# Dealing out a search step's maxima and a layer norm's sums, and letting GpSimd's differences run four batches behind

## What is computed

```python
# ctx_4096: (16, 1601, 2048), channel map; x: (16, 64, 2048)
k = 38                                   # of the 64 channels of x
_, topk_idx = jax.lax.top_k(cm, k)
mask = jnp.zeros((B, L, C), x.dtype).at[b_idx, l_idx, topk_idx].set(1.0)
crucial_features = crucial_channels * x
subcrucial_features = subcrucial_channels * x
c_max = jnp.max(crucial_features, axis=1, keepdims=True)
s_max = jnp.max(subcrucial_features, axis=1, keepdims=True)
...
x = x + _L0_xattn_ref(_layernorm(x, axis=-1), ctx_4096, ...)
```

## Time and profile before

| | us |
|---|---|
| median of three runs | 2584.66 (2582.23 to 2588.15) |
| profiled execution, its own time | 2591.74 |
| its span, first to last instruction | 2589.9 |
| search | 0 to 838 |
| flags, two rows done again | 838 to 916 |
| maxima stage | 916.4 to 996.7 |
| convolution, gates, attention, feed-forward | 996.7 to 2589.9 |

### The profile page before, as it was taken

How to read it: one execution, slowest core, us unless ns; L and a number is a source line. 1 busy time by engine, 2 the same in 40 slices (tenths; PEclk the granted TensorE clock), 3 DMA queues, 4 the chain that set the end, 5 groups by cost and what they waited for, 6 DMA issues and landing times. The chain is left out here.

```text
span 2589.9 us, 38980 instructions
## 1 busy us (share of the span) xinstructions
PE 2071.0 (80%) x15304; PEld 1714.1 (66%) x15304; DVE 1415.6 (55%) x2152; ACT 1023.5 (40%) x2002; POOL 968.0 (37%) x874
## 2 busy tenths in 40 slices
PE   4668678677776021558999999999999989989999
PEld 3555557566666021546887787888777767878887
DVE  5777879887888789572244464014444451651000
ACT  5665757666665023351223233222322322332222
POOL 1111111111110043266555554555554534544544
PEclk8888889888998565778999999999999999999999
DMA  8886767678884010224222444432224435434443
GB/s 323 299 302 233 274 209 273 234 259 282 284 280 144 25 65 0 77 89 151 85 82 76 153 139 125 127 98 82 78 79 158 139 98 193 139 102 131 140 153 111
DMA packets 141062, 407.67 MB, mean 157 GB/s; under 512 B 15184, under 2 KB 27728, under 8 KB 139728
## 3 DMA queue, kind: packets, MB, share of 16 engines
q1 hardware_dynamic: 140592, 403.55, 46.3%
q0 software_dynamic: 288, 1.64, 0.2%
HBM read 379.96 MB, written 25.17 MB: 156 GB/s over the span
## 5 line engine op out<-in xcount | busy, mean ns | idle before, releaser
L1059 POOL TENSOR_TENSOR t<-t,t 128x512 fp32r<-128x512 f32 (+1 forms) x488 | 643.4, 1329 | 627.6 <-ACT t L1052 627.3
L1593 PE MATMUL ps<-t,t 128*128 128x512 f32 x1856 | 744.8, 401 | 46.4 <-POOL t L1059 43.7
L1594 PE MATMUL ps<-t,t 128*128 128x512 f32 x1856 | 729.2, 393 | 0.0
L1595 PE MATMUL ps<-t,t 128*128 128x512 f32 x1856 | 729.0, 393 | 0.0
L683 PE MATMUL ps<-t,t 128*128 128x128 bf16 (+1 forms) x6656 | 486.1, 237 | 242.9 <-DVE t L435 233.8
L683 PEld LDWEIGHTS ps<-t,t 128*128 128x128 bf16 x6656 | 447.5, 109 | 314.1 <-DVE t L435 266.3
L1052 ACT ACTIVATE t<-t 128x512 fp32r<-128x512 f32 (+1 forms) x488 | 295.5, 608 | 750.7 <-PE ps L1595 478.6
L435 DVE TENSOR_SCALAR t<-t,t 128x1601 bf16<-128x1601 f32 x512 | 513.5, 1052 | 31.0 <-PE ps L683 27.1
L645 ACT ACTIVATE t<-t,t 128x1601 bf16<-128x1601 f32 x256 | 416.9, 1628 | 89.6 <-DVE t L595 84.4
L1593 PEld LDWEIGHTS ps<-t,t 128*128 128x128 f32 x1856 | 352.3, 190 | 130.2 <-POOL t L1059 36.1
L1595 PEld LDWEIGHTS ps<-t,t 128*128 128x128 f32 x1856 | 352.1, 190 | 75.7
(11 more groups left out here) (205 smaller groups left out, 1788.3 us busy)
## 6 DMA issues: line engine op xcount, KB each, us to landing
t<-ctxT SPq DMA_DIRECT2D x256, 800.5 KB, 5.7
t<-wqkv SPq DMA_DIRECT2D x192, 256.0 KB, 3.2
t<-wo SPq DMA_DIRECT2D x128, 256.0 KB, 4.5
t<-wb SPq DMA_DIRECT2D x128, 256.0 KB, 3.4
t<-xT SPq DMA_DIRECT2D x32, 256.0 KB, 6.1
t<-xT SPq DMA_DIRECT2D x2, 4096.0 KB, 12.4
x1d<-t SPq DMA_DIRECT2D x8, 1024.0 KB, 5.5
t<-x1d SPq DMA_DIRECT2D x32, 256.0 KB, 4.8
```

The lines of the kernel that those rows point to most:

```text
L1059: e.tensor_tensor(wlo[r][:, 0:nk, :], raw[r][:, 0:nk, :], wh[r][:, 0:nk, :].bitcast(F32), ALU.subtract).then_inc(w_lo, 1)
L1593: e.matmul(bank[:, :], wh[r][:, q, :], xl, start=(kt == 0), stop=False)
L1594: e.matmul(bank[:, :], wlo[r][:, q, :], xh, start=False, stop=False)
L1595: m = e.matmul(bank[:, :], wh[r][:, q, :], xh, start=False, stop=(c == NCH[p] - 1 and q == nk - 1))
```

## The change

A quad's maxima come in two pairs. `maxima(0)` and `bounds(0)`, for the tiles 4i and 4i+1, stay at the head of the step; `maxima(1)` and `bounds(1)`, for 4i+2 and 4i+3, stand behind the mask c0. (In steps 0 and 1, with no mask c, they stand ahead of the third mask.) The bounds and ties are written for two tiles at a time, so that they take two instructions each a step instead of one, and ScalarE's signs 0 and 1 wait for the first half's bounds, 2 and 3 for the second's. ScalarE reads the fourth count of the step before behind its first sign instead of ahead of it, count 0 behind sign 2, and counts 1 and 2 behind sign 3.

The 16 matmuls of the layer norm's sum are dealt over four steps, 14 to 17 and 26 to 29, four a step; all that follows in the layer norm starts two steps later.

In the maxima stage GpSimd's difference b waits for product b+3 (before: product b), VectorE takes the rest's maximum four batches behind the product instead of two, behind the product's own maximum, and the four sums of batches 12 to 15 stand at the end. No buffer is added.

```diff
-    LN0_SUM, LN0_SUB, LN0_VAR, LN0_MUL, LN0_XSUM = (15, 27), (17, 29), (22, 34), (24, 36), (28, 44)
+    LN0_SUM, LN0_SUB, LN0_VAR, LN0_MUL, LN0_XSUM = (17, 29), (19, 31), (24, 36), (26, 38), (30, 46)
...
-            if i == LN0_SUM[h] and u == 0:
+            if LN0_SUM[h] - 3 <= i <= LN0_SUM[h]:
+                t = 4 * (i - LN0_SUM[h] + 3) + u
                 e.wait_ge(d_x[h], 16 * NT)
                 if h:
                     e.wait_ge(ln0_var, h)
-                for t in range(NT):
-                    m = e.matmul(ps[7][:, :], ones, XN[:, h, t, :], start=(t == 0), stop=(t == NT - 1))
-                m.then_inc(ln0_total, 1)
+                m = e.matmul(ps[7][:, :], ones, XN[:, h, t, :], start=(t == 0), stop=(t == NT - 1))
+                if t == NT - 1:
+                    m.then_inc(ln0_total, 1)
...
+            def maxima(half):
+                if half == 0 and b >= 2 and t0 == 0:
                     e.wait_ge(fin, NF * (b - 1))
-                for _, u in quad:
+                for u in (2 * half, 2 * half + 1):
                     landed(e, 4 * i + u)
                     e.max(v8[:, y, t0 + u, :], ring[(4 * i + u) % NR][:, 0:C]).then_inc(maxed, 1)
+
+            def bounds(half):
+                n, two = 4 * i + 2 * half, slice(t0 + 2 * half, t0 + 2 * half + 2)
+                e.wait_ge(maxed, n + 2)
+                e.tensor_scalar(nT[:, n:n + 2], v8[:, y, two, 3], TINY, -1.0, ALU.max, ALU.mult).then_inc(bound4, 1)
+                e.tensor_tensor(eqb[y][:, two, :], v8[:, y, two, 0:7], v8[:, y, two, 1:8], ALU.is_equal).then_inc(tied, 1)
+            if i < NQ:
+                maxima(0)
...
-            done = 1
+            done = 2
+            if i == 0 or i == 1:
+                maxima(1)
+                bounds(1)
             for k, (kind, u) in enumerate(masks_of(i)):
...
                 done += 1
-                if first_steps and i <= NQ + 1 and done < 7:
-                    end_batch([done])
+                if 2 <= i < NQ and done == 3:
+                    maxima(1)
+                    bounds(1)
+                if first_steps and i <= NQ + 1 and done <= 7:
+                    end_batch([done - 1])
...
-        e.wait_ge(bound4, i + 1)
+        e.wait_ge(bound4, 2 * i + u // 2 + 1)
...
-            if 2 <= i:
-                counts_scalar(e, i - 1, 3)
             for u in range(4):
                 if i < NQ:
                     sign_scalar(e, i, u)
                 ln0_scalar(e, i, u)
-                if 1 <= u and 1 <= i <= NQ + 1:
-                    counts_scalar(e, i, u - 1)
+                if u == 0 and 2 <= i:
+                    counts_scalar(e, i - 1, 3)
+                if 1 <= i <= NQ + 1:
+                    for v in {2: [0], 3: [1, 2]}.get(u, []):
+                        counts_scalar(e, i, v)
...
+    LAG = 4
...
+        def total(b):
+            e.tensor_reduce(stat[:, 2, b, :], crc_of(b), AX.X, ALU.add).then_inc(v_sums, 1)
...
         for b in range(B):
             e.tensor_tensor(crc_of(b), M8[:, b, :, :], xn_of(b), ALU.mult).then_inc(crucial, 1)
-            if b >= 2:
-                rest(b - 2)
             e.wait_ge(crucial, b + 1)
             e.tensor_reduce(stat[:, 0, b, :], crc_of(b), AX.X, ALU.max)
-            if b - 1 in BY_DVE:
-                e.tensor_reduce(stat[:, 2, b - 1, :], crc_of(b - 1), AX.X, ALU.add).then_inc(v_sums, 1)
-        rest(B - 2)
-        e.tensor_reduce(stat[:, 2, B - 1, :], crc_of(B - 1), AX.X, ALU.add).then_inc(v_sums, 1)
-        rest(B - 1)
+            if b >= LAG:
+                rest(b - LAG)
+        for b in range(B - LAG, B):
+            total(b)
+            rest(b)
...
         for b in range(B):
-            e.wait_ge(crucial, b + 1)
+            e.wait_ge(crucial, min(b + LAG, B))
```

More of the change, by code:

```diff
@@ L576, in end_batch @@
                     fin_vector(e, bf, s)
-            quad = [(i, u) for u in range(4)] if i < NQ else []
             b, t0 = tile_of(4 * i)
-            y, four = b % 2, slice(t0, t0 + 4)
-            if i < NQ:
-                if b >= 2 and t0 == 0:
+            y = b % 2
+            def maxima(half):
+                if half == 0 and b >= 2 and t0 == 0:
                     e.wait_ge(fin, NF * (b - 1))
-                for _, u in quad:
+                for u in (2 * half, 2 * half + 1):
                     landed(e, 4 * i + u)
                     e.max(v8[:, y, t0 + u, :], ring[(4 * i + u) % NR][:, 0:C]).then_inc(maxed, 1)
+            def bounds(half):
[5 more added lines that the diff above has]
+                maxima(0)
             if 1 <= i <= NQ:
@@ L593, in search_vector @@
             if i < NQ:
-                e.wait_ge(maxed, 4 * i + 4)
-                e.tensor_scalar(nT[:, 4 * i:4 * i + 4], v8[:, y, four, 3], TINY, -1.0, ALU.max, ALU.mult).then_inc(bound4, 1)
-                e.tensor_tensor(eqb[y][:, four, :], v8[:, y, four, 0:7], v8[:, y, four, 1:8], ALU.is_equal).then_inc(tied, 1)
+                bounds(0)
             if 1 <= i <= NQ:
                 e.wait_ge(a_dec, g + 1)
-                e.wait_ge(tied, g + 1)
+                e.wait_ge(tied, 2 * g + 2)
                 w = insA[:, 4 * g:4 * g + 4].rearrange("p (a n) -> p a n", n=1).to_broadcast([128, 4, 3])
@@ L634, in search_vector @@
                 e.wait_ge(fin, NF * (B - 1))
-                e.wait_ge(bound4, NQ)
+                e.wait_ge(bound4, 2 * NQ)
                 flags_vector(e, 0, 0, B - 1)
```

## The result

The changed kernel takes 2459.5 us (median of 4, 2458.7 to 2460.6) against 2586.1 (four runs): 0.9512 of the time before, interval 0.9496 to 0.9529, 126.6 us less. The forecast was 2489.3 with 2462 to 2525. The profiled execution took 2460.0 us, its span is 2456.9, against 2591.7 and 2589.9 before. So the two profiles lie 133.0 us of span apart where the medians lie 126.6: for the most part because the profiled execution before was 5.6 us slower than its median and the one after 0.5.

What follows compares the result with a forecast made beforehand. VectorE's search and maxima stages, slowed mainly by MAX8 waits for late ring tiles, were taken as the bound. Search -84 and maxima -11.4 give -95.4 us, from the median 2584.7 to 2489.3, range 2462 to 2525.

Steps and rivals of the forecast that it cites:

- wait for the ring, start left out: Search: VectorE's MAX8 waits 127.9 us for refilled tiles; all but 17 us at the start goes, 111 us.
- its return by busier DMA: Search: loads at 357 GB/s take about as long as VectorE's shortened step, so 22 us of wait come back, bounds 5 and 64.
- new instructions: Search: two more instructions a step and one more turn from maximum to bounds cost 0.3 us a step, 19 us, bounds 13 and 26.
- layer norm's sum (with L511): Search: dealing TensorE's block of matmuls over steps removes 24.1 us of waits, 4 given back, so 20 us go.
- fourth count: Search: ScalarE's count behind sign 0 is ready at 2.65 us, wanted at 2.7; costs 6 us, bounds 0 and 20.
- maxima stage: Stage on VectorE and GpSimd: cycle of 3.57 us instead of 4.7, GpSimd's code load paid behind the wait; 11.4 us go.
- all that follows: The rest of the kernel outside search and maxima stage: no term in the forecast's sum, so 0.
- The 17 us of the start: Start of the search, where the ring fills: 17 us of VectorE's wait for tiles can't go.
- The load of GpSimd's code: Maxima stage: load taken as paid behind the wait, first difference at 932.3; load in the shadow, chance 0.35, worth 5.8 us.
- The pace of the maxima stage: Maxima stage: 0.14 + 2.34 + 1.09 = 3.57 us a batch, with the product held by GpSimd's running difference.
- the rival's place: Slower rival: VectorE's decision behind b1 waits for ScalarE's late fourth count, up to 122 us, time 2611; chance 0.04.
- everything hides: Rival: little DMA wait, no count wait, 13 us for instructions, GpSimd's load in the shadow; 2454 at most, 2462 middle; chance 0.20.

Runs made afterwards that it cites:

- the stage alone: The kernel before with only the changed code of the maxima stage set in, the search left as before: 2565.0 us, 0.9909 of the kernel before.
- experiment 3: The changed kernel with all four maxima and both bounds at the head of the step again: 2551.8 us, 0.9862 of the kernel before.
- Experiment 4: Two variants of the changed kernel: a ring of 13 buffers instead of 14, 2481.7 us; masks, signs and counts over 801 of 1601 values, 2253.7 us.
- Experiment 6: The changed kernel with GpSimd's difference waiting for the product six or three batches on instead of four: 2454.5 and 2454.2 us.
- experiment 2: The changed kernel with the 16 matmuls of the layer norm's sum in one block again: 2478.4 us, 0.9579 of the kernel before.
- Experiment 5: The changed kernel with ScalarE reading the fourth count ahead of sign 0 again: 2446.9 us, 0.9456 of the kernel before.

## Why the forecast was right and where it was not

The forecast took 95.4 us off the profiled span and off the median alike; 133.0 went from the span and 126.6 from the median. Term by term, by the profiles:

| term | forecast | profile |
|---|---|---|
| wait for the ring, start left out | -111 | -110.8 |
| its return by busier DMA | +22 | 0 |
| new instructions | +19 | +11 |
| layer norm's sum (with L511) | -20 | -23.3 |
| fourth count | +6 | +10.7 |
| maxima stage | -11.4 | -18.1 |
| all that follows | 0 | -2.5 |

The 11 for the instructions is what is left of the 112.4 when the waits are taken off (-110.8, -26.0, +2.7, +10.7, -0.3); VectorE's busy time in the search rose from 660.9 to 670.1 (up to 725.8 us, as far behind the last mask as 838 before), by 9.2. Such a remainder is worth a few us at most: the search of before ended 3.2 us earlier in the profile of the stage alone, and the changed search's last mask starts anywhere from 718.9 to 725.8 in the five profiles that have it unchanged.

**Bound and mechanism** were right. VectorE waited for tiles, and the place of the second pair decided it (experiment 3). The 17 us of the start came out too (16.2 before 60 us, 17.1 in all).

**The return of the ring's wait** is the step that failed most, "I take 0.6 us a step for some 23 such steps and 0.2 for 40: 22 us". It took the 357 GB/s at a share of 0.94 for what the DMA engines can give, found 10.2 us of loads beside 10.0 us of VectorE's work, and priced the tie at 0.6 us a step. That window was a mean over stretches with and without loads under way (in slices of 1.1 us its rate goes from 0 to 444 GB/s). Experiment 4 shows 409 GB/s, and the changed kernel itself 412, so the same loads take 8.9 us. The steps did take 10.2 us, but with 0.9 us of wait for tiles in all behind the start. The queueing that the forecast feared was there, 7.0 us a refill instead of 6.4 from 60 to 180 us, and stayed inside the margin that the new place gives; in the steps behind, the refill took 5.4 us (median from 180 to 640 us). The forecast's lower bound of 5 was still too high. By the Trainium skill (DMA: Bandwidth & Descriptors, Latency and other measured facts), a refill might have taken up to 7.6 us, by the prediction's estimate; the trace's medians of 7.0 in the changed kernel and 8.1 with the engines full don't tell such a latency from queueing.

**The load of GpSimd's code** is the second step that failed: "I take it that the load is paid behind the wait". I had chosen between two readings by their nearness to a third case, the start of the kernel, where other code is loaded. Experiment 6 decides for the one that I gave 0.35: the load runs in the shadow, and 17.2 us was the right sum; 18.1 were measured. The Trainium skill's figure (GPSIMD Engine Reference, Instruction dispatch), about 6 us at the first call without the wait, does not hold here: the gap is 8.55 to 9.4 us from the request, and nothing is left to pay when the wait is longer (0.09 us in experiment 6).

**The pace of the maxima stage**, 3.50 to 3.53 us a batch, came out near the forecast's 3.57, but not by its sum. That had each product held for 1.09 us by GpSimd's running difference. Only the product of 813.52 is (2.35 us); the later ones take 1.21 to 1.24: each starts about when the difference beside it ends. The 3.5 us are VectorE's own three instructions, so the nearness is luck.

**The new instructions** cost some 0.18 us a step and not 0.3, under my lower bound if the remainder is taken as it stands. They cost little beside the maxima: from the MAX8 of 693.38 to the mask behind it pass 0.61 us, for two maxima, bounds and ties, and one of the batch's small steps.

**The layer norm's sum** came out near its size, and at the fast clock as taken: the granted clock is 1.00 in the steps 14 to 17 and 0.96 in 26 to 29. Alone it is worth 17 to 19 us (experiment 2), as the dealt matmuls delay the fourth count, which the forecast had not seen.

**The fourth count** was the rival's place, and its reserve of 0.05 us was indeed none: 12.1 us of waits, 10.7 more than before, inside the bounds of 0 and 20. Experiment 5 gives back 12 to 14.

The time lies below the range because the rival "everything hides" was right in three of its four parts (the tiles, GpSimd's load, the instructions) and wrong only in the count, and I left out half of it. The 2.5 us by which all that follows got shorter are of the size by which executions differ, and no forecast of mine.

## What to carry to other kernels

Where a ring's refill is late by a fixed return, the point of use can be moved instead of adding a buffer: look in the order for work that needs nothing new and can stand between. Read the capacity of a queue from a stretch in which it alone sets the pace, never from a mean over a stretch with waits; and read the time of a refill from the stretch where the load is highest, not from a median over all. And when one wait goes, look for the next reserve near zero: here a count read one instruction too late cost about a tenth of the gain.

## What the runs showed of the hardware

GpSimd's load of code takes 8.55 to 9.4 us from the request, and in parallel to whatever its next instruction waits for. DMA engines with some five loads under way (an estimate: 53 tiles of 8.1 us and 18 pieces of x of 7.8 in 120 us) gave 409 GB/s beside busy engines. The median load of 800 KB took 6.4 us from issue at 292 GB/s, 7.0 at 360 and 8.1 at 409. The granted clock of the search rose from 0.88 to 0.96 with the same matmuls, while TensorE's waits for masks fell from 233.8 to 155.4 us.
